# Two attentions of a four-layer kernel: pairing the narrow products on TensorE

## What is computed

```python
scores = jnp.einsum('bhtd,bhsd->bhts', Q, K) * scale
scores = jnp.where(mask, scores, -inf)
attn = jax.nn.softmax(scores, axis=-1)
out = jnp.einsum('bhts,bhsd->bhtd', attn, V)
```

## Time and profile before

| | |
|---|---|
| profiled execution, its own time | 6028.71 us |
| its span | 6026.9 us |
| median of three runs | 6026.17 us |
| attention 1, first shifted score to last narrow products | 2009.30 to 2728.78 us |
| attention 3, the same | 4537.39 to 5464.89 us |
| TensorE busy, whole span | 5352.1 us (89%) |
| VectorE busy | 3558.0 us (59%) |
| ScalarE busy | 2765.7 us (46%) |
| GpSimd busy | 1470.6 us (24%) |
| maxima of pieces (VectorE) | 2304, 1190.2 us |
| exponentials (ScalarE) | 1920, 993.5 us |
| narrow products, values | 3840, 510.9 us |
| narrow products, denominators | 1920, 266.1 us |

### The profile page before, as it was taken

One profiled execution on the slowest core, in us unless ns is written; L12 is line 12 of the kernel. 1 busy time (PEld: TensorE's weight loads), 2 busy tenths in 40 slices (PEclk: granted clock), 3 DMA queues, 4 the chain that ended last, 5 costly groups with the idle time before them and its releaser, 6 DMA issues. The chain is left out here.

```text
span 6026.9 us, 69068 instructions
## 1 busy us (share of the span) xinstructions
PE 5352.1 (89%) x26050; PEld 1878.7 (31%) x26050; DVE 3558.0 (59%) x4608; ACT 2765.7 (46%) x5261; POOL 1470.6 (24%) x708
## 2 busy tenths in 40 slices
PE   6987999999697999996788888886879999997999
PEld 2333333434233233322222222222323333322444
DVE  4548777877342777750588888881137777761010
ACT  2423333333122466662377777773215666663111
POOL 0004333334000466660000000000005666662000
PEclk8988999999799899998799999998979999998999
DMA  3233333333221322313111111112234232302000
GB/s 107 96 103 103 96 84 87 91 95 88 82 70 38 80 63 62 73 31 110 42 28 30 32 29 28 30 22 85 75 77 80 53 71 58 66 26 98 21 21 14
DMA packets 459769, 383.48 MB, mean 64 GB/s; under 512 B 169809, under 2 KB 359094, under 8 KB 458764
## 3 DMA queue, kind: packets, MB, share of 16 engines
q1 hardware_dynamic: 459428, 379.00, 23.4%
HBM read 242.83 MB, written 135.14 MB: 63 GB/s over the span
## 5 line engine op out<-in xcount | busy, mean ns | idle before, releaser
L2174 DVE TENSOR_REDUCE att_part<-att_scores 128x1 f32<-128x423 f32 (+1 forms) x2304 | 1190.2, 579 | 425.9 <-PE att_scores L2021 424.6
L2138 ACT ACTIVATE att_prob<-att_scores 128x512 f32<-128x512 f32 (+1 forms) x1920 | 993.5, 601 | 549.1 <-PE att_scores L2033 548.6
L2157 POOL TENSOR_TENSOR att_acc<-att_acc,att_prob 128x1024 f32<-128x1024 f32 (+1 forms) x416 | 984.7, 2367 | 441.3 <-ACT att_prob L2138 439.2
L2481 DVE TENSOR_REDUCE att_part<-att_scores 128x2 f32<-128x802 f32 x1024 | 964.6, 988 | 161.9 <-PE att_scores L2385 155.7
L2467 ACT ACTIVATE att_prob<-att_scores 128x512 f32<-128x512 f32 (+1 forms) x1664 | 861.4, 602 | 252.2 <-PE att_scores L2399 250.4
L2021 PE MATMUL att_scores<-att_k,att_q 97*128 97x423 f16 (+1 forms) x2304 | 816.5, 358 | 84.4 <-DMA att_q<-in_c_q 60.4
L2033 PE MATMUL att_scores<-att_q,att_k 98*128 98x512 f16 (+1 forms) x1920 | 721.5, 383 | 13.6 <-ACT att_prob L2138 13.4
L1264 POOL TENSOR_TENSOR scan_z<-scan_r,scan_states 128x512 f32<-128x512 f32 x256 | 410.1, 1602 | 1107.8 <-DVE scan_states L1297 1092.7
L2157 POOL TENSOR_TENSOR att_acc<-att_prob 128x1024 f32<-128x1024 f32 x32 | 75.6, 2364 | 2443.2 <-ACT att_prob L2138 2443.2
L2399 PE MATMUL att_scores<-att_q,att_k 49*128 49x512 f16 (+1 forms) x1664 | 471.7, 390 | 110.1 <-ACT att_prob L2467 109.9
L2044 PE MATMUL att_sums<-att_prob,att_v 128*32 128x512 f32 (+1 forms) x3840 | 510.9, 604 | 0.0
(11 more groups left out here) (294 smaller groups left out, 6103.3 us busy)
## 6 DMA issues: line engine op xcount, KB each, us to landing
v<-scan_val SPq DMA_DIRECT2D x96, 256.0 KB, 2.3
att_v<-v SPq DMA_DIRECT2D x32, 768.0 KB
att_spread<-recips SPq DMA_DIRECT2D x64, 256.0 KB
mix_plane<-in_mask SPq DMA_DIRECT2D x16, 800.5 KB, 6.6
att_k<-k1hi SPq DMA_DIRECT2D x32, 400.2 KB
att_k<-k3hi SPq DMA_DIRECT2D x32, 400.2 KB
scan_x<-in_ctx_t SPq DMA_DIRECT2D x12, 1024.0 KB, 8.9
o<-att_out SPq DMA_DIRECT2D x32, 256.0 KB, 2.1
```

Of the source, the lines that this page charges most:

```text
L2138: nc.scalar.activation(prob[g % NP][0:kw(kt), h, :], scores2[0:kw(kt), n % RING2, :], ACT.Exp).then_inc(exped, 1)
L2157: nc.gpsimd.tensor_tensor(acc[s % 2][0:kw(kt)], so_far[0:kw(kt), 0:PH, :], prob[g % NP][0:kw(kt), 0:PH, :], ALU.add).then_inc(padded, 1)
L2174: nc.vector.reduce_max(part[q % 2][:, hc, piece:piece + 1], scores1[:, bank["piece", p], 0:PIECE], AX.X).then_inc(reduced, 1)
L2481: nc.vector.reduce_max(part[q % 2][:, :, ec, piece], scores1[:, bank["unit", p], :, 0:PIECE], AX.X).then_inc(reduced, 1)
```

## The change

In both attentions:

- `mix` of two neighbouring tiles is issued together, behind the shifted scores of an odd tile or of the last tile, immediately ahead of `count` of the same two tiles. Each such block has 12 narrow products (8 of values, 4 of denominators); the tile between has none. The last tile of a round, NT being odd, keeps a block of its own.
- There are five buffers `prob` in place of four.
- The pieces due are worked out by slot: each tile has five slots, one behind each of the four shifted scores and one behind the narrow products, and a slot is left empty once in 65 (attention 1) or once in 17 (attention 3). Before, it was always the last slot of a tile that stayed empty. The sum per tile is as before. The wait of ScalarE for the transposed maxima follows the same count.

```diff
--- before.py
+++ after.py
@@ -1850,19 +1850,20 @@
     PIECES = -(-NK // T)
     PIECE = -(-NK // PIECES)
     UNITS = QUAD * C * PIECES
-    RING1, RING2, NB, NP = 3, 3, 4, 4
+    RING1, RING2, NB, NP = 3, 3, 4, 5
     LEAD, TURN, LAG = 5, 6, 2
     AHEAD = UNITS + LEAD * UNITS // NT
     PH = 2
     PADDS = NT - 1
     PAIRS = -(-NT // 2)
+    SLOTS = QUAD + 1
     LOADS = 2 * len(HALF) + 1 + (len(HALF) if latents else 0)
     VLOADS = 3 if latents else 2
     CLEARED = 2 + (NB if latents else 0)
 
-    def pieces_by(g):
-
-        return min(N * UNITS, AHEAD + (g + 1) * UNITS // NT)
+    def pieces_by(g, slot=QUAD):
+
+        return min(N * UNITS, AHEAD + (g * SLOTS + slot + 1) * UNITS // (NT * SLOTS))
 
     def turn_after(q):
 
@@ -2077,13 +2078,14 @@
                             pe.wait_ge(topsent[s % 2], 16 * (s // 2 + 1))
                         for h in range(QUAD):
                             shift(s, kt, h)
-                            if issued < pieces_by(g):
+                            while issued < pieces_by(g, h):
                                 next(one)
                                 issued += 1
                     if g >= LAG:
                         ms, mk = divmod(g - LAG, NT)
-                        mix(ms, mk)
                         if mk % 2 or mk == NT - 1:
+                            for m in range(mk - mk % 2, mk + 1):
+                                mix(ms, m)
                             count(ms, mk)
                     while g < G and issued < pieces_by(g):
                         next(one)
@@ -2136,7 +2138,7 @@
                         n = g * QUAD + h
                         act.wait_ge(shifted, n + 1)
                         nc.scalar.activation(prob[g % NP][0:kw(kt), h, :], scores2[0:kw(kt), n % RING2, :], ACT.Exp).then_inc(exped, 1)
-                        while rounds < N and turn_after(rounds) <= min(pieces_by(g), pieces_by(g - 1) + (h if h < QUAD - 1 else UNITS)):
+                        while rounds < N and turn_after(rounds) <= pieces_by(g, h if h < QUAD - 1 else QUAD):
                             round_top(rounds)
                             rounds += 1
                 drain(N - 1)
```

## The result

The changed kernel takes 6110.59 us (median of 4 runs, 6097.5 to 6115.1) against 6025.11 for the kernel before: a ratio of 1.0128, with a 95% interval of 1.0106 to 1.0151. It is slower by 85 us where 57 were forecast. A second set of runs gave 6099.64 against 6028.86, ratio 1.0107 (1.0085 to 1.0129), 71 us. The two sets differ by the granted clock of their executions; the experiments come back to it.

What follows compares the result with a forecast made beforehand. TensorE was taken to bound the kernel, 98% busy while pieces, scores and narrow products run together. Merging saves 49 us, longer stretches lose 106, so 6026.2 + 57 = 6083 us; range 6010 to 6125, the forecast's own 6050 to 6117.

Steps and rivals of the forecast that it cites:

- The mechanism: Ten-slot stretches of attentions 1 and 3: three banks and VectorE's pace make TensorE wait; plain loss 0.58 and 0.66 us.
- The saving: Narrow blocks of attentions 1 and 3: merging two mixes saves 0.22 us each, 224 merges, 49 us.
- The rival with 0.32: Changes between wide and narrow products: a merge saves 0.32 us, 72 us in all, 6024 to 6060; chance 0.17.
- the one with 0.08: Paired block: only the entry is saved, 18 us in all, giving 6114 us; chance 0.10.
- Fast rival: Second half of ten-slot stretches: VectorE's idle time absorbs the waits, only 49 us saved remain, 5977 us; chance 0.13.
- The sum: Whole kernel: 49 us saved by merges against 106 us lost in longer stretches, +57 us.
- With pieces: Stretches of attentions 1 and 3 while pieces last: losses of 35 + 60 = 95 us before the saving.
- Without pieces: Rest of the attentions, only scores: 0.34 us net a pair, 0.56 before the saving, some 19 pairs, 11 us.
- Elsewhere: Stages other than attentions 1 and 3: unchanged, 0 us.
- The range: Whole time: forecast's own range 6050 to 6117 us, from losses of 73 to 140 less 49; text's range 6010 to 6125.
- Five buffers: Exponentials in attentions 1 and 3: fifth buffer costs nothing; without it ScalarE would wait up to a block.
- Slots spread: Empty slots of pieces in both attentions: effect inside the stretch sums; ScalarE's transpose wait nothing, at most 32 x 0.3 = 10 us.

Runs made afterwards that it cites:

- half maxima: Each piece's maximum taken over half its columns, in both kernels: kernel before 5970.42 us, changed kernel 5974.69 us.

## Why the prediction was right, and where it was off

**The mechanism** was the forecast's: three banks, VectorE every 0.48 us, so that TensorE waits from the sixth piece of a stretch on. Start of block 4.18 after the first piece, block 2.72, pair 6.90 were forecast; 4.18, 2.71 and 6.89 are in the trace. The counter-test, half maxima, took the loss in the two attentions from 73 to 9 us (in the medians from 85 to 4).

**The saving**, 0.22 us a merge, was 0.24 where nothing else held the stretch. The rival with 0.32, which would have made the change about even, and the one with 0.08 both fall. By the Trainium skill (TensorEngine Tiling (Array Packing), Key Properties) changing the tiling mode drains TensorE. The trace agrees that going in and out has a price, these 0.24 us; whether a drain makes it, or that the narrow products are fp32 and the others fp16, no run here tells apart.

**Fast rival** (VectorE's idle time takes up the longer stretch): wrong for the reason given. VectorE is idle for longer, 1.98 us, and only in the block.

**The sum** was 28 us short in the first set of runs and 14 in the second. In the profiled executions three terms were too small:

- *With pieces*, 61 us against 50. In attention 1 the stretch with the transpose took 7.63 us in every full round, where 6.94 now, less the 0.22 saved, plus the 0.70 of the sum make 7.42. Its beginning in the changed kernel, first TensorE's piece, then VectorE:

```profile
2314.39 0.35 PE L2022 MATMUL att_scores<-att_k,att_q 97*128 97x401 f16 x1
...
2314.77 1.06 DVE L2176 TENSOR_REDUCE att_part<-att_scores 128x1 f32<-128x401 f32 x2 [1.98 <-PE att_scores L2022]
2315.86 0.22 DVE L2181 TENSOR_REDUCE att_top<-att_part 128x16 f32<-128x64 f32 x1
2316.00 3.99 DVE L2176 TENSOR_REDUCE att_part<-att_scores 128x1 f32<-128x401 f32 x8
```

  Behind the second piece VectorE makes the round's maxima out of those of its pieces (0.22 us). The sum counts the bank that the transpose takes and has no term for this reduction. It stands in a chain without slack: the third piece's reduction starts 1.23 us after the first, where two steps are 0.97, so 0.26 late, and the stretch is 0.21 longer than the sum had it. No run took it out by itself. The 0.21 make 3 of the 11 us. The stretch beside the multiplication and the short one behind it took 10.20 together where the sum makes 10.10, one more of the 11. In attention 3 the stretch with transpose and multiplication took 8.53 us (5043.12 to 5051.65) where 5.47 + 2.72 = 8.19 were forecast, and once 10.0, with a clock of 0.70 in its block. The multiplication is not the cause: it lasts 1.05 us there (5046.82). The round's maxima stand in this chain too (0.24 us, at 5044.65). The last piece (5048.44) waits for the reductions behind the multiplication, as forecast, but comes 0.11 late, and the block does not come 0.26 us later:

```profile
5048.44 0.35 PE L2022 MATMUL att_scores<-att_k,att_q 97*128 97x423 f16 x1 [0.98 <-DVE att_part L2176]
5048.63 0.38 PE L2034 MATMUL att_scores<-att_q,att_k 98*128 98x512 f16 x1
5048.94 1.92 PE L2045 MATMUL att_sums<-att_prob,att_v 128*32 128x512 f32 x16
```

  A score stands between them, and the block comes 0.50 after the piece. That is 0.24 of the 0.34, and the 0.34 make 4 of the 11 us. The other stretches of a round came within 0.1 us of the sum: in attention 3 the plain ones took 7.07, the one with the total 8.08, the one behind it 6.57 (6.79 in a single round), the one with invert 6.88.
- *Without pieces*, 12 us against 7. The stretch was right at the full clock (a pair in 6.16 us), but some windows there were not at it. The changed kernel in attention 3, ten us each:

```profile
5470.00:5480.00 10.00, 8.43 (x50) 2.14 (x52) 3.56 (x8) 5.36 (x12) 6.45 (x4) 0.85 0.15 53
5490.00:5500.00 10.00, 8.82 (x50) 2.17 (x49) 0.00 (x0) 7.58 (x16) 5.16 (x3) 1.00 0.01 2
5500.00:5510.00 10.00, 8.96 (x43) 2.04 (x46) 0.00 (x0) 6.15 (x13) 6.63 (x4) 0.83 0.00 1
5520.00:5530.00 10.00, 8.59 (x45) 2.16 (x48) 0.00 (x0) 7.04 (x15) 8.00 (x4) 0.91 0.07 27
```

  A block that took 1.74 us up to its denominators took 2.77, 3.16 and 3.27 there, and one in attention 1 took 3.35 (2715.48). The four make some 6 us. Before, the whole of attention 1's such stretch was at 1.00. I had not considered the clock in the tails.
- *Elsewhere*, 13 us against 0. "The rest unchanged" was true of the code; the profiled executions differ in the clock at the end of attention 2, and at like mean clocks the kernels differ by the attentions' share alone. That 85 us lie nearer to the range's end than to the forecast is in part this chance.

**The range.** Its low end is worked out wrongly, without effect: 205 x 0.37 less 0.61 in 14.6 rounds is 67, where the prediction says 70 and further down 73.

**Five buffers.** The step "without cover it would be a wait of up to a block" was wrong: with four, nothing is lost.

**Slots spread.** "Taken alone it would be no change" failed for attention 1: 8.9 us. Where the empty slot lies decides whether a piece waits behind the multiplication. The stretch sums had that gain (-0.61) for the pair but the sentence on the part alone did not; and paired, the spread is worth 28 us in attention 1 (7 of them by the clock), so the change without it would have been slower still.

## What to carry to other kernels

Merging work of the busiest engine saves its changes of mode, but it also lengthens the stretches in which that engine feeds the others; the number of buffers between them says how long a stretch may be (here three banks and steps of 0.40 against 0.48 us: five pieces, not six). Count from the first item after a gap until the receiver's lag reaches the depth of the ring; an idle share of 26% on the receiver is no reserve if the ring cannot carry work into it. Count every operation of the receiver in that chain, short ones too. And a long operation of the receiver, like the multiplication here, is worth moving to another engine before anything is merged: it gave 11.6 us in attention 3 here. No run tried the pairing with the multiplication moved, or with a fourth bank, so whether the pairing pays then is not shown.

## What was not expected of the hardware

The same VectorE multiplication of 128x512 fp32, two SBUF operands and an SBUF result, takes from 0.68 us to over 2.2 us. Its median over 32 is 977 ns before, 1050 in the changed kernel and 2185 with half maxima; the last is this row of the view of its line (count, ns min/median/max, first and last start):

```profile
L2198 DVE TENSOR_TENSOR att_out<-att_sums_sb,att_spread x32: 680/2185/2240, 2069.9 to 5411.6; 128x512 f32<-128x512 f32 x32
```

The timelines of GpSimd and VectorE around one multiplication say why. Before:

```profile
2322.55 2.37 POOL L2157 TENSOR_TENSOR att_acc<-att_acc,att_prob 65x1024 f32<-65x1024 f32 x1 [1.32 <-ACT att_prob L2138]
...
2324.43 1.04 DVE L2196 TENSOR_TENSOR att_out<-att_sums_sb,att_spread 128x512 f32<-128x512 f32 x1
```

Changed:

```profile
2331.06 2.35 POOL L2159 TENSOR_TENSOR att_acc<-att_acc,att_prob 65x1024 f32<-65x1024 f32 x1 [2.34 <-ACT att_prob L2140]
...
2332.51 1.44 DVE L2198 TENSOR_TENSOR att_out<-att_sums_sb,att_spread 128x512 f32<-128x512 f32 x1
```

Changed, with half maxima:

```profile
2331.35 2.35 POOL L2159 TENSOR_TENSOR att_acc<-att_acc,att_prob 65x1024 f32<-65x1024 f32 x1 [1.62 <-ACT att_prob L2140]
...
2332.01 2.23 DVE L2198 TENSOR_TENSOR att_out<-att_sums_sb,att_spread 128x512 f32<-128x512 f32 x1
```

GpSimd's sum ends at 2324.92, 2333.41 and 2333.70; the multiplication at 2325.47, 2333.95 and 2334.24, each time 0.54 or 0.55 us later, however early it was issued. It reads as if it stood still until GpSimd's instruction is over, and then took what is left of its own work. The same distance is in the other traces: 0.55 us in the pairing without the spread (2345.48 + 1.45 against 2344.03 + 2.35). All the traces with the multiplication on VectorE say it, 384 multiplications in 12 runs. The 330 that start inside one of GpSimd's sums end 0.55 us after it (two of them 0.58 and 0.63); the 43 that meet none take 0.68 to 0.69 us. In the other 11 VectorE came first: it takes its 0.69, and GpSimd's sum up to 2.89 instead of 2.36. The maxima out of PSUM run beside GpSimd's sums at their old length (medians 566 and 589 ns before, 565 and 589 after).

By the Trainium skill (SBUF — State Buffer, Who interferes with whom) a VectorE instruction with two SBUF inputs takes its second through a read interface that it shares with GpSimd, and whichever of the two comes second waits for the whole of the first, while one with at most one SBUF input, outside the two-port modes, does not contend. The traces agree, by the counts above, and in the maxima. What no run tried is a whole kernel with the multiplication on VectorE and GpSimd's sums taken away. The price of such an instruction is then not its duration in a row but where it falls: from 0.68 us to 0.55 us plus what is left of GpSimd's 2.36. The prediction took 1.04 us for it wherever it stood. In the changed kernel that held in attention 3 (median of 16: 1046 ns, 974 before) and not in attention 1 (1453 against 1032). With half maxima it did not hold at all: 2180 ns in attention 3 where the unpaired kernel with the same maxima has 1195, one microsecond in each of 16 rounds, in the very stretch that makes some 17 of the 21 us by which the pairing still loses there. No run took it out by itself. With the multiplication on GpSimd VectorE has no such wait left.
